# Linear attention in a decoder layer: the query side computed with tokens on the partitions and unsplit float32 operands, then turned back

## The reference, cut to what matters

```python
q = elu(x @ Wq.T) + 1;  k = elu(x @ Wk.T) + 1;  v = x @ Wv.T       # split in 16 heads of 32
kv_state = einsum('bhnd,bhne->bhde', k, v);  k_state = k.sum(axis=2)
attn_out = einsum('bhnd,bhde->bhne', q, kv_state)
denom = maximum(einsum('bhnd,bhd->bhn', q, k_state), 1e-6)[..., None]
out = (attn_out / denom + local) @ Wp.T + bp      # local: a convolution of three taps over tokens
```

## Time and profile before

| | |
|---|---|
| median of 3 runs | 3194.57 us (3193.95 to 3194.88) |
| profiled execution, its own time | 3195.02 us |
| span of that execution | 3193.3 us |
| PE busy | 3140.6 us, 98% of the span |
| DVE, ACT, POOL busy | 1802.6, 1381.9, 1019.7 us |
| chain that ended last | PE 94%, DVE 2%, ACT 1%, POOL 1% |
| mean granted clock of PE | 0.995 of full speed |

### The profile page before, as it was taken

The page is one execution under the profiler, slowest core; times in us unless marked ns, Lnnn a source line. Parts: engine busy times, 40 slices in busy tenths (PEclk is TensorE's granted clock), DMA queues, the critical chain, the costliest instruction groups (busy, mean ns, idle before and its releaser), DMA issues.

```text
span 3193.3 us, 40644 instructions
## 1 busy us (share of the span) xinstructions
PE 3140.6 (98%) x15508; PEld 2630.7 (82%) x15508; DVE 1802.6 (56%) x3737; ACT 1381.9 (43%) x2635; POOL 1019.7 (32%) x838
## 2 busy tenths in 40 slices
PE   7999999999989999999999999999999999999998
PEld 6888888888877888888888877888888888888887
DVE  5666575766668788788778767223222232221354
ACT  4444444444446676666666653212222122221243
POOL 1332323233247666666666650000000000000144
PEclk9999999999999999999999999999999999999999
DMA  3112121111231212222121131100001000010386
GB/s 109 40 40 80 40 80 40 64 56 40 80 126 56 81 67 68 71 77 68 54 94 68 54 119 67 53 27 27 27 27 53 27 27 27 27 52 18 124 291 217
DMA packets 118705, 220.73 MB, mean 69 GB/s; under 512 B 7408, under 2 KB 13552, under 8 KB 118512
## 3 DMA queue, kind: packets, MB, share of 16 engines
q1 hardware_dynamic: 118512, 218.14, 20.1%
HBM read 152.06 MB, written 66.06 MB: 68 GB/s over the span
## 4 chain that ended last, share of the span: by engine, by line
PE 94%; DVE 2%; ACT 1%; issue 1%; POOL 1%; DMA 0%; POOLq 0%; ACTq 0%; DVEq 0%
PE c_p L132 11%; PE c_p L130 11%; PE c_p L131 11%; PE a_p L130 6%; PE a_p L131 6%; PE a_p L132 6%; PE b_n L130 4%; PE b_n L132 4%; PE b_n L131 4%; PE b_t L1593 3%; PE a_r L132 2%; PE a_r L130 2%; PE a_r L131 2%; PE d_p L130 2%; PE d_p L132 2%; PE d_p L131 2%
## 5 line engine op out<-in xcount | busy, mean ns | idle before, releaser
L1213 POOL TENSOR_SCALAR b_soft<-b_soft,b_one_in_sum 128x512 f32<-128x512 f32 x256 | 401.0, 1568 | 305.3 <-DVE b_one_in_sum L1396 305.3
L1813 ACT ACTIVATE c_gate<-c_p,c_bias 128x512 f32<-128x512 f32 x180 | 124.0, 689 | 718.4 <-PE c_p L132 718.4
L1847 DVE TENSOR_TENSOR c_gate<-c_gate,c_gate 128x512 f32<-128x512 f32 x64 | 44.3, 692 | 524.2 <-ACT c_gate L1813 524.2
L344 POOL TENSOR_TENSOR kept_scale<-c_ln_ve,minus_half 128x4 f32<-128x4 f32 x16 | 16.1, 1009 | 896.5 <-DVE c_ln_ve L336 896.5
L1415 DVE TENSOR_TENSOR b_p_lo<-b_t,b_p_hi 128x512 fp32r<-128x512 f32 x256 | 175.3, 685 | 167.0 <-ACT b_p_hi L1270 164.5
L1261 ACT ACTIVATE b_soft<-b_soft,b_minus_top 128x512 f32<-128x512 f32 x256 | 185.1, 723 | 190.3 <-DVE b_minus_top L1407 185.7
L570 ACT ACTIVATE a_elu<-a_p 128x512 f32<-128x512 f32 x128 | 76.6, 599 | 332.1 <-PE a_p L132 285.3
L1270 ACT ACTIVATE b_p_hi<-b_t 128x512 fp32r<-128x512 f32 x256 | 151.4, 591 | 107.8 <-PE b_t L1593 107.8
L1407 DVE CUSTOM_DVE_ANT_0 b_soft<-b_l,b_mask_row 128x512 f32<-128x512 f32 x256 | 175.3, 685 | 0.0
L2033 POOL TENSOR_TENSOR d_x<-d_x,d_y 128x512 f32<-128x512 f32 x64 | 85.1, 1332 | 266.0 <-ACT d_y L2050 266.0
L1593 PE MATMUL b_t<-ident,b_soft 128*128 128x128 f32 x1024 | 156.7, 276 | 11.5 <-DVE b_p_lo L1415 11.0
(11 more groups left out here) (309 smaller groups left out, 10004.2 us busy)
## 6 DMA issues: line engine op xcount, KB each, us to landing
a_x<-in_x SPq DMA_DIRECT2D x16, 1024.0 KB, 8.2
a_res<-in_x SPq DMA_DIRECT2D x16, 1024.0 KB, 6.3
x<-a_res SPq DMA_DIRECT2D x16, 1024.0 KB, 5.2
b_mem<-in_ctx SPq DMA_DIRECT2D x16, 1024.0 KB, 5.4
b_x<-x SPq DMA_DIRECT2D x16, 1024.0 KB, 5.6
b_res<-x SPq DMA_DIRECT2D x16, 1024.0 KB, 5.5
x<-b_res SPq DMA_DIRECT2D x16, 1024.0 KB, 4.5
c_x<-x SPq DMA_DIRECT2D x16, 1024.0 KB, 5.9
```

The lines of the kernel that those rows point to most:

```text
L1213: pool.tensor_scalar(soft[:, at, :], soft[:, at, :], one_in_sum[:, at:at + 1], None, ALU.mult).then_inc(p_norm.sem, p_norm.unit)
L1813: act.activation(gate[j % 2][i][:, :], gating.banks[(3 * j + i) % 6][:, :], ACT.Tanh if g == "c" else ACT.Sigmoid, bias=added[:, i, j:j + ...
```

## The change

The query and the masked state stay unsplit float32. The attention is computed with a 128x128 piece of the query (features by tokens) as the stationary operand and the state of 132 columns as the moving one, so that tokens lie on the partitions: 128 columns of sums and 4 columns of denominators, one for each head of the tile. There are 16 such matmuls (T times C), three of them to a bank, in six groups. For each group DVE clamps the 12 denominators, inverts them, and multiplies the sums with them, spread by a broadcast pattern. Then PE turns the 16 blocks of 128x128 back, four to a bank, and DVE adds `local` straight from PSUM. The order on PE is `attend(t)` ahead of each key tile and `turn_att(c)` behind each value tile. On DVE the groups stand around elu's back, group 4 and 5 ahead of tiles 2 and 3 of the next tokens' statistics.

Gone are: the split of query and state, the denominators' product, their split, the spread and its copy, the table for it, and POOL's part in query and sum. Both lists of banks are now `Rota`s, in which a job's bank rotates from step to step, without the two filler jobs of `first`; the key tiles' banks are freed by other events than before. The state matmuls have 132 columns instead of 130.

```diff
-        KVW = P + HEADS
+        KVW = P + HC
+        BLOCKS, IN_BANK = C * T, 3
+        GROUPS = -(-BLOCKS // IN_BANK)
...
-            first = Ring(self.banks(held, "a_p", 5),
-                         [(rden_f, 0, 1)] + [(elu_out, t) for t in range(T)]
-                         + [(v_sb, t) for t in range(T)] + [(elu_out, T + c) for c in range(C)]
-                         + [(kv_part, 2), (kv_part, 5)] + [(tap2, c, -1) for c in range(C)] + [(kv_part, 5)], B)
+            first = Rota(self.banks(held, "a_p", 5),
+                         [(elu_out, t, 0) for t in range(T)] + [(v_sb, t, 0) for t in range(T)] + [(elu_out, T + c, 0) for c in range(C)]
+                         + [(kv_sb, g, 0) for g in range(2)] + [(tap2, c, -1) for c in range(C)], B)
-            second = Ring(self.banks(held, "a_r", 3),
-                          [e for c in range(C) for e in ((spread_sb, c, 1), (att_sb, c, 1))]
-                          + [(x1_sb, t, 1) for t in range(T)], B)
+            second = Rota(self.banks(held, "a_r", 3),
+                          [(att_sb, g, 1) for g in range(GROUPS)] + [(z_f, c, 1) for c in range(C)] + [(x1_sb, t, 1) for t in range(T)], B)
...
 gpsimd:
-                        for c in range(C):
-                            pool.wait_ge(att_sb.sem, att_sb.upto(old.b, c))
-                            pool.tensor_tensor(att[c % 2][:, :], att[c % 2][:, :], local[old.par][:, c, :], ALU.add)
...
-                            pool.tensor_tensor(q[new.par].low[:, c, :], elu[:, c % 2, :],
-                                                       q[new.par][:, c, :].high_f32(), ALU.subtract)
...
 vector:
+                    def attend(g):
+                        n, blocks = len(blocks_of(g)), slice(blocks_of(g)[0], blocks_of(g)[-1] + 1)
+                        bank = second.bank(s, ATT + g)[:, 0:n * KVW].rearrange("p (i e) -> p i e", i=n)
+                        dve.wait_ge(att_ps.sem, att_ps.upto(old.b, g))
+                        dve.tensor_scalar(rden[:, blocks, :], bank[:, :, P:KVW], 1e-6, None, ALU.max)
+                        dve.reciprocal(rden[:, blocks, :], rden[:, blocks, :])
+                        dve.tensor_tensor(heads(att[:, blocks, :]), heads(bank[:, :, 0:P]),
+                                          rden[:, blocks, :].unsqueeze(3).broadcast_to([P, n, HC, HD]), ALU.mult)
                     if old:
-                        dve.wait_ge(den_ps.sem, den_ps.upto(old.b))
-                        dve.tensor_scalar(rden[:, :], first.banks[0][0:HEADS, :], 1e-6, None, ALU.max)
-                        dve.reciprocal(rden[:, :], rden[:, :])
+                        attend(0)
                     if new:
                         elu_back(0)
+                    if old:
+                        attend(1)
+                        attend(2)
+                        attend(3)
+                    if new:
+                        elu_back(1)
                     if after:
                         self.norm_tile(dve, N, after, x, 0)
                         self.norm_tile(dve, N, after, x, 1)
                     if new:
-                        elu_back(1)
+                        elu_back(2)
                     if old:
-                        dve.tensor_tensor(rden_s[LOW:LOW + HEADS, :], rden[:, :], rden_s[0:HEADS, :].bitcast(F32), ALU.subtract)
+                        attend(4)
+                        attend(5)
                     if after:
                         self.norm_tile(dve, N, after, x, 2)
                         self.norm_tile(dve, N, after, x, 3)
...
+                            dve.tensor_tensor(z_sum[c % 2][:, :], second.bank(s, TURNED + c)[:, :], local[old.par][:, c, :], ALU.add)
...
+                            dve.tensor_tensor(kv[:, 2 * g:2 * g + 2, :], bank, kv_mask[:, :, :], ALU.mult)
...
 tensor:
-                        for c in range(C):
-                            pe.wait_ge(q_lo.sem, q_lo.upto(old.b, c))
-                            mm = product(pe, den_bank[:, :], kv[old.par][:, c * KVW + P:c * KVW + 2 * P],
-                                         q[old.par][:, c, :], c == 0, c == C - 1)
+                    def attend(t):
+                        for c in range(C):
+                            g, i = divmod(t * C + c, IN_BANK)
+                            if t == 0 and c == 0:
+                                pe.wait_ge(elu_out.sem, elu_out.upto(old.b))
+                                pe.wait_ge(kv_sb.sem, kv_sb.upto(old.b))
+                            if i == 0 and (freed := second.freed(s, ATT + g)):
+                                pe.wait_ge(*freed)
+                            mm = pe.matmul(second.bank(s, ATT + g)[:, i * KVW:(i + 1) * KVW], q[:, c, t * P:(t + 1) * P], kv[:, c, :], start=True, stop=True)
+
+                    def turn_att(c):
+                        if freed := second.freed(s, TURNED + c):
+                            pe.wait_ge(*freed)
+                        pe.wait_ge(att_sb.sem, att_sb.upto(old.b))
+                        for t in range(T):
+                            mm = pe.transpose(second.bank(s, TURNED + c)[:, t * P:(t + 1) * P], att[:, t * C + c, :], self.ident[:, :])
                     if new is None:
-                        for c in range(C):
-                            self.b_turn_memory(pe, c)
+                        for t in range(T):
+                            attend(t)
+                            if t:
+                                self.b_turn_memory(pe, t - 1)
+                        self.b_turn_memory(pe, C - 1)
                     if new:
                         for t in range(T):
+                            if old:
+                                attend(t)
                             (key tile t)
...
-                            pe.matmul(bank[:, :], head_rows[:, c, :], rden_s[:, :], start=True, stop=True)
-                            product(pe, bank[:, :], kv[old.par][:, c * KVW:c * KVW + P], q[old.par][:, c, :], True, True)
                         (value tile c)
+                        if old:
+                            turn_att(c)
```

More of the change, by code:

```diff
@@ L456, in first_masks @@
[L456 to L467, removed]
@@ L589, in values @@
                         act.activation(v1[:, t, :, 0:P],
-                                               first.bank(V + t)[:, :].rearrange("p (c e) -> p c e", c=C), ACT.Copy).then_inc(v_sb.sem, v_sb.unit)
+                                               first.bank(new.b, V + t)[:, :].rearrange("p (c e) -> p c e", c=C), ACT.Copy).then_inc(v_sb.sem, v_sb.unit)
                     def z_high(c):
@@ L643, in step @@
                         middle_tap(new.b + 1, 0)
[L644 to L647, removed]
-                                                kv_f, ACT.Copy).then_inc(kv_hi.sem, kv_hi.unit)
                     if new and new.b == B - 1:
@@ L660, in tokens_high @@
                         act.wait_ge(kq_ps.sem, kq_ps.upto(b - 1))
-                    act.activation(xT.high[:, c, :], first.bank(TURN + c)[:, :], ACT.Copy).then_inc(xT_hi.sem, xT_hi.unit)
+                    act.activation(xT.high[:, c, :], first.bank(b - 1, TURN + c)[:, :], ACT.Copy).then_inc(xT_hi.sem, xT_hi.unit)
                 def middle_tap(b, c):
-                    act.activation(local[b % 2][:, c, :], first.bank(TURN + c)[:, :], ACT.Identity,
+                    act.activation(local[b % 2][:, c, :], first.bank(b - 1, TURN + c)[:, :], ACT.Identity,
                                    bias=conv_b[:, c:c + 1], scale=conv_w[:, c, 1:2]).then_inc(tap1.sem, tap1.unit)
@@ L692, in elu_back @@
                         dve.wait_ge(elu_exp.sem, elu_exp.upto(new.b, 2 * u + 1))
-                        bank = kq_bank(u)
+                        bank = kq_bank(new.b, u)
                         if u < T:
@@ L730, in step @@
                         self.norm_tile(dve, N, after, x, 3)
-                    if new:
-                        elu_back(2)
-                        weight_low(WQ, 0)
-                    if after:
                         self.norm_variance(dve, N, after)
+                    if new is None:
+                        for c in range(C):
+                            self.b_memory_low(dve, c)
                     if new:
@@ L790, in tokens_low @@
                     dve.wait_ge(tap1.sem, tap1.upto(b, c))
-                    dve.tensor_tensor(xT.low[:, c, :], first.bank(TURN + c)[:, :], xT[:, c, :].high_f32(), ALU.subtract).then_inc(xT_lo.sem, xT_lo.unit)
+                    dve.tensor_tensor(xT.low[:, c, :], first.bank(b - 1, TURN + c)[:, :], xT[:, c, :].high_f32(), ALU.subtract).then_inc(xT_lo.sem, xT_lo.unit)
                 def outer_taps(b, c):
-                    bank, loc = first.bank(TURN + c), local[b % 2]
+                    bank, loc = first.bank(b - 1, TURN + c), local[b % 2]
                     dve.scalar_tensor_tensor(out=loc[:, c, 1:S], in0=bank[:, 0:S - 1], scalar=conv_w[:, c, 0:1],
@@ L817, in output @@
                     pe.wait_ge(*freed)
```

(16 more changed lines are left out.)

165 lines of the change are left out of this document (60 added, 105 removed).

## The result

| | before | after |
|---|---|---|
| median | 3194.73 us (3193.95 to 3195.07, 4 runs) | 3169.95 us (3169.25 to 3170.44, 4 runs) |
| ratio, 95% interval | | 0.9923 (0.9905 to 0.994) |
| span of the profiled execution | 3193.3 us | 3168.7 us |

What follows compares the result with a forecast made beforehand. PE, busy 98%, was taken as the bound: 36.4 us (steps 2 to 15) + 2.5 + 2 + 4.5 (steps 0, 1, 16) = 45.4 us off 3195.0, so 3149 us for the median; range 3142 to 3160.

Steps and rivals of the forecast that it cites:

- the price of the attention on PE: PE, steady step: each attention group of four matmuls costs 0.54 us, four of them 2.16 us.
- Rival B: Attention matmuls on PE: true FP32 takes four passes, a step gains 0.8 us, total 20 us, 3174 us; chance 3%.
- Rival A: Attention matmuls on PE: stationary loads don't overlap, 0.20 us each instead of 0.112, 3165 us; chance 9%.
- C: Rival: the ends of the phase give nothing, only the steady steps' 36.4 us are gained, 3158 us; chance 8%.
- E: Rival: transposes among the values let PE's clock fall, one half-clock stretch takes a step's gain, 3186 us; chance 3%.
- The 6.58 us taken away: PE, steady step: denominators (2.79 us) and spreads with the old attention matmuls (3.79 us) leave the stream.
- the turned group's 0.44: PE, steady step: four transposes back cost 0.35 + 0.09 = 0.44 us, four groups 1.76 us.
- The cover before the turned tile: Steady step: DVE ends its groups at 13.4 us, PE wants them at 15.8 for the first turned tile, slack 2.4.
- D: Rival: DVE's groups come late, PE waits before a turned tile, kernel turns slower, 3208 us; chance 2%.
- Step 0: Start of the phase: the first key tile's bank waits for nothing, gain 2.5 us, between 1.8 and 3.2.
- Step 1: PE runs ahead without denominators and meets DVE's last token split; gain 2 us, from 0 to 3.7.
- Step 16: End of the phase: PE passes the `b_x` wait at +22 to +25 instead of 28.1; gain 4.5 us, 3 to 6.

Runs made afterwards that it cites:

- The FP32R run: Changed kernel with query and masked state written and read as unsplit FP32R, low parts dropped from the attention: 3142.07 us, ratio to before 0.9835.
- the run with the statistics first: Changed kernel with VectorE taking the next tokens' statistics ahead of groups 2, 3, 4 and 5: 3174.27 us, ratio to before 0.9935.

## Why the prediction was wrong

**The step that failed** is the price of the attention on PE: "An attention group of four is 4 x 0.112 + 0.09 ... = 0.54 us", and before it "32 of them from 392.10 to 395.67, 0.112 us each". The row said x32; the code beside it has 16 calls. The 0.112 us was the price of a record, and a call is two. I took the price of a record from the trace and the number of calls from the diff. Two errors stand in the 0.54: four records too few, 0.45 us, and the return's 0.09 counted twice, which took a fifth of that back. With 0.90 instead of 0.54 four groups cost 3.60 instead of 2.16; by the forecast's own sum, with the 0.03 that the state's two columns took, the gain is 6.58 - 1.76 - 3.60 - 0.03 = 1.2, measured 1.05. The 0.14 between them is at the long matmuls right behind a group, of which the second and third start about a hundredth late too: the four attention groups with the key tiles take 14.53 us (344.40 to 358.93), less 10.90 for the 48 long ones 3.63; the turned groups with values and queries take 23.65 (358.93 to 382.58), less 21.8 for the 96 long ones 1.87. With these 6.58 - 1.87 - 3.63 - 0.03 is the 1.05 measured. Times 14, the error is 20 to 22 us, all of the miss. The FP32R run, with one record a call, took the time down to 3142. The forecast had named its own sign of being wrong, "starts 0.2 or more apart in the attention": from call to call they are 0.225.

**Rival B came out.** It had 3%, 0.8 us a step and 3174 us; the kernel took 3170. It was dismissed with "the trace's unsplit float32 matmul of 130 columns at 0.112 us speaks against it", the same misreading. Its 0.8 us a step doesn't come out of the terms beside it either: 6.58 - 1.76 - 3.74 - 0.06 is 1.0, and 0.7 with 0.09 for each return. The Trainium skill, FP8 and Floating Point Precision, TensorE Precision Notes, gives four passes for true FP32; the trace agrees at 512 columns (0.86 us against 4 x 0.227 = 0.91 by that rule) and at 132 (0.225 against 0.234). At 66 columns it doesn't: 0.22 against 0.12, where the price of the record holds. At 132 the agreement proves little, since there an FP32R record costs the same 0.113 as a float32 one, and not half of it: the price by passes and the price by the record meet at this width.

**Rival A** (exposed loads) gave 3165, 5 us from the result, with a mechanism that isn't there in that form: the state's matmuls and the attention's cost the same for each record. **C** fell: the ends gave 9.9 us. **E**, the clock, fell too: from 361 to 374 us, with the transposes among the values, the granted clock is 1.00.

**What held.** The 6.58 us taken away, with which the step's sum closes, and the turned group's 0.44 (0.47 with all that is late behind it). DVE's group at 1.0 us (0.95). The cover before the turned tile came out at 2.6 us for 2.4, but by luck: both ends of it were off by more, the last group done 14.6 us into the step instead of 13.4, and the turned tile due at 17.3 instead of 15.8, since the attention took longer on PE. No wait in a steady step, so nothing for D; the run with the statistics first shows that D's mechanism is real, and starts at a nearer place than forecast. Step 0 at 3.2 is at the edge of its range, 1.8 to 3.2; the wait for tap 1 was its cause. Step 1 gained 1.1: as forecast, it meets DVE's token splits, in three waits here (3.0 us together), with a stretch at the lower level of the clock behind them (mean granted clock 0.53 from 72 to 78 us, 0.50 in the same stretch before). Step 16 passed `b_x` at +22.5, within 22 to 25, and gained 5.6. The sum for the three ends was 9.0, measured 9.9.

## What to carry to other kernels

A price from the trace and a count from the code go together only if one call is one record: divide the group's count by the loop's count first. An unsplit float32 matmul is two records here and costs nearly as much as four FP32R ones at 512 columns (3.8), so it is no saving against a split in three. On narrow operands, where each record costs its floor of 0.11 us, its two records should be cheaper than the split's three, about 0.23 against 0.34 at 132 columns; that is reckoned from the prices, no run split the attention in this layout. Where groups hand banks back to PE, put the work that can wait for a DMA behind them, and compute the cover for each bank, not only for the last consumer, with the wait for the DMA in it.

## What the runs showed of the hardware

One call of an unsplit float32 matmul shows as two records with two loads; an FP32R matmul or a float32 transpose shows as one. With a stationary piece of 128x128 a record costs about 0.11 us: in float32 at 66 and at 132 columns, in FP32R at 132, in a transpose of 128, and in runs of 4, 8 or 16. At 512 columns a float32 record costs 0.43 and an FP32R one 0.227. The longer start distance behind short matmuls (0.32 instead of 0.227) is no fee for changing over: runs of twice the length, half as many, took the same time.
